# Row pairs folded ahead of the W transform, and both mixings of a spectral block kernel in plain fp32 on 128- and 64-value blocks

## The chip, the core and the metric

The kernel runs on one core of one Trainium2 chip. The metric is device time in microseconds (us) of one launch. Engines are named as in the profile: PE is TensorE, PEld its weight loads, DVE is VectorE, ACT is ScalarE, POOL is GpSimd, SP is the engine that issues most DMAs. Each runs its own instruction list in order, and they meet at semaphores. SBUF is the working memory; PSUM, with 8 banks of 512 fp32 values in each of 128 partitions, takes what PE writes and is not read by POOL.

## The reference

Input x has the shape (4, 128, 128, 768) in fp32: batch, H, W, channels. The 768 channels are 8 blocks of 96, and each block has its own complex 96 x 96 weights.

```python
xf = jnp.fft.rfft2(x, axes=(1, 2), norm='ortho')       # 128 x 65 complex modes
xf = xf.reshape(b, h, wf, NUM_BLOCKS, BLOCK)           # 8 blocks of 96
o1r = relu(xr @ w1[0] - xi @ w1[1] + b1[0])            # the first mixing
o1i = relu(xi @ w1[0] + xr @ w1[1] + b1[1])
o2r = o1r @ w2[0] - o1i @ w2[1] + b2[0]                # the second mixing
o2i = o1i @ w2[0] + o1r @ w2[1] + b2[1]
xc = softshrink(o2r, 0.01) + 1j * softshrink(o2i, 0.01)
out = jnp.fft.irfft2(xc, s=(128, 128), axes=(1, 2), norm='ortho') + x
```

## The kernel before

The work is 32 items, one for each pair of channel block and image (8 x 4). An item is an image of 128 x 128 x 96, which fills one of two buffers `x0` and `x1`, with W on the partitions. The engines loop over 16 steps of two items each (`Fori(0, STEPS)`, the body written out for both items). The order on every engine is written by hand; no scheduler moves anything. An item q goes through five stages on PE.

1. **Forward lines** (`lines(q, p, 0)`, PE line L351). For each of the 96 channels one matmul multiplies a 128 x 128 matrix of x (W by H), as the weights, by the cosine and sine table of W. It goes by 26 groups of up to 4 channels. ACT (L485) or DVE (L592) first packs a group of x, whose values lie 96 apart, into a ring of four slots; after the matmuls ACT (L494) or DVE (L601) moves the group from PSUM to `ydg`.
2. **Mixing**. 22 units of three W frequencies (the first has two). Per unit: `fwd_h` (L372), six matmuls with 96 x 128 weights and 130 columns, transforms H with only 65 of the 128 frequencies, once for the real and once for the imaginary part; DVE puts the full set together from sums and differences (L629 to L632). `mix1` takes three real products in place of four, each of them as three matmuls on numbers split in a high and a low part of type fp32r (L389, L390, L391), for which ACT and POOL make the parts (L513, L519, L734, L743, L746). DVE combines (L652, L655), ACT applies bias and relu (L536). `mix2` (L425, L427) takes two matmuls of 192 columns for each frequency, the bias b2 being a 97th row of the weights. DVE shrinks into `ydg` (L673, L675). At the end `merge` unites W frequencies 0 and 64.
3. **Inverse lines** (`lines(q, p, 1)`, again L351, L485, L494, L592, L601): as the forward ones, with `ydg` as source and destination.
4. **Rows** (`rows`, L445 and L448): 13 groups of two matmuls with up to 480 columns; ACT copies half of the results (L583), DVE and POOL add and subtract them with x (L684, L688, L690, L752) in place.
5. SP stores the buffer in pieces as DVE finishes them, then loads the image after next into it.

In PE's list a plain fp32 matmul is two instructions with a weight load each, a high and a low pass; an fp32r one is a single instruction.

The packing of the next item's first groups stands on ACT behind the last `vcopy` copy of this item, and on DVE behind the last `finish`.

Of the kernel before, what the change touches and what calls it, by code (L numbers as in the profile page):

```python
# [12 lines left out]
NB = 8  # L13
# [3 lines left out]
HS = H // 2 - 1  # L17
KW = W // 2 + 1
# [4 lines left out]


CG = 4
# [5 lines left out]
RING = 4  # L31


def packer(g):
    return "act" if g < 2 or g % 2 == 0 else "dve"


def packed_count(g, who):
    return sum(packer(i) == who for i in range(g + 1))


PACKED = {who: packed_count(NG - 1, who) for who in ("act", "dve")}

KU = 3
NU = 1 + (KW - 2) // KU

# [5 lines left out]
WEIGHT_DMAS = 6  # L52


LAG1, LAG2 = 2, 3


WHOLE = (0, 1)
SPLIT = [v for v in range(NU) if v not in WHOLE]
DVE_SPLITS = (2,)  # L60
POOL_SPLITS = [v for v in SPLIT if v not in DVE_SPLITS]

SUM_LAST = 0

LOW_BANKS = (NU - 3, NU - 1)

# [3 lines left out]
for _name, _n in (("fwd_w", W), ("fwd_h", 2 * HC), ("inv_h", H), ("inv_w_even", W), ("inv_w_odd", W),  # L70
                  ("merge_even", H), ("merge_odd", H)):
    COLS[_name] = (_at, _at + _n)
    _at += _n
TABLE = _at


def transform_table():

# [18 lines left out]
    fwd_w[:, 3::2] = -sin(n, kw)  # L99
    half = np.arange(0, 65)  # L100
    fwd_h = np.concatenate([cos(n, half), sin(n, half)], 1)
# [15 lines left out]
    return np.concatenate([fwd_w / 128, fwd_h, inv_h, inv_even / 128, inv_odd / 128,  # L117
# [3 lines left out]
def build(nc, x, w1, b1, w2, b2, table, out):  # L121
    with ExitStack() as ctx:
# [3 lines left out]
        def sem(name):  # L126
# [3 lines left out]

        xs = [sb(f"x{p}", [W, H, CB]) for p in range(PAIRS)]

        ydg = sb("ydg", [128, 128, CB])


        w1i = sb("w1i", [CB, CB])
        w1g = sb("w1g", [CB, 3, CB])
        w1hi = sb("w1hi", [CB, 3, CB], F32R)  # L140
        w1lo = sb("w1lo", [CB, 3, CB], F32R)
        b1s = sb("b1s", [CB, 2])
        w2r = sb("w2r", [CB + 1, 2, CB])
        w2i = sb("w2i", [CB, 2, CB])
        pcopy = [sb(f"pcopy{j}", [CB, KU, 2 * HC]) for j in range(2)]

        z_or_packed = sb("z_or_packed", [128, 2 * 3 * KU * H])
        z = [z_or_packed[0:CB, j * 3 * KU * H:(j + 1) * 3 * KU * H].rearrange("p (a k n) -> p a k n", a=3, k=KU)
             for j in range(2)]
        packed = [z_or_packed[:, j * CG * 128:(j + 1) * CG * 128].rearrange("p (c k) -> p c k", c=CG)  # L150
                  for j in range(RING)]
# [56 lines left out]


        T_BANK, R_BANK, I_BANK, M_BANK = 2, 3, 4, 5  # L210
        E_BANK = T_BANK

        M_STEP = 320

# [555 lines left out]
```

## Time and profile before

| | us |
|---|---|
| median of 3 runs | 5806.42 (5803.06 to 5810.91) |
| the profiled execution | 5807.0 |
| its span on the core | 5805.2 |
| first matmul of the program, from the span's start | 28.6 |
| PE busy in the span | 5558.5 (96%) |
| DVE, ACT, POOL busy | 4148.0, 3751.7, 3055.2 |

The profiled execution lies 0.6 us above the median, 0.01% of it, so that sums made against the profile can be set against the median as they are. The item's stages repeat 32 times; what one stage costs is read from the start of its first matmul to the start of the next stage's first. A matmul's own duration in the records is longer than the distance to the next one, because matmuls overlap in the array; the distance between starts is what counts.

### The profile page before, as it was taken

What the parts mean: (1) busy time and instruction counts of PE and PEld (TensorE: products, weight loads), DVE (VectorE), ACT (ScalarE), POOL (GpSimd) and SP (SyncE); (2) the same over time, 40 slices, a digit from 0 to 9 for tenths busy, and PEclk for the clock granted to TensorE, in tenths of its full rate; (3) what the DMA queues carried; (4) which work ended last, traced back from release to release, by engine and by line L of the source; (5) the groups of instructions that cost most, each with busy time, mean ns of one, the idle gap of its engine ahead of it and who ended that gap; (6) DMA issues with size and microseconds to landing.
All of it is one profiled execution on the core that took longest, in us unless ns stands there. A gap on an engine that the chain in (4) does not pass through costs nothing.

```text
span 5805.2 us, 115095 instructions
## 1 busy us (share of the span) xinstructions
PE 5558.5 (96%) x36736; PEld 5058.7 (87%) x36736; DVE 4148.0 (71%) x8579; ACT 3751.7 (65%) x6288; POOL 3055.2 (53%) x2420
## 2 busy tenths in 40 slices
PE   7999999999999999999999999999999999999999
PEld 7888988889888898888988888888889888898888
DVE  5777677676777777777777777677776777767676
ACT  5666666666666666666666666666666666666665
POOL 4445564455644556544555446554465544555445
PEclk9999999999999999999999999999999999999999
DMA  4331233312333213332133331333312333123311
GB/s 92 88 89 45 46 88 88 90 48 42 88 88 90 57 38 84 88 90 64 39 76 88 90 72 37 70 88 90 81 37 60 88 90 88 39 51 88 90 45 44
DMA packets 1070797, 413.95 MB, mean 71 GB/s; under 512 B 1069920, under 2 KB 1070048, under 8 KB 1070176
## 3 DMA queue, kind: packets, MB, share of 16 engines
q1 hardware_dynamic: 1070176, 406.13, 29.8%
q8 instruction: 334, 5.47, 0.4%
q14 instruction: 287, 2.35, 0.1%
HBM read 204.76 MB, written 201.33 MB: 70 GB/s over the span
## 4 chain that ended last, share of the span: by engine, by line
PE 82%; issue 12%; DVE 4%; ACT 1%; POOL 1%; DMA 0%; SPq 0%; DVEq 0%; ACTq 0%; POOLq 0%
PE ps L351 20%; PE ps L372 16%; PE ps L425 11%; PE ps L427 11%; PE ps L389 6%; PE ps L390 6%; PE ps L391 6%; PE ps L445 3%; PE ps L448 3%; DVE x L690 2%; PE ps L387 2%; ACT z_or_packed L485 1%; DVE clamped L673 1%; DVE x L688 1%; DVE ydg L601 0%
## 5 line engine op out<-in xcount | busy, mean ns | idle before, releaser
L351 PE MATMUL ps<-tab,z_or_packed 128*128 128x128 f32 x12288 | 1476.1, 285 | 199.3 <-ACT z_or_packed L485 195.1
L351 PEld LDWEIGHTS ps<-tab,z_or_packed 128*128 128x128 f32 x12288 | 1459.0, 200 | 237.7 <-ACT z_or_packed L485 228.6
L752 POOL TENSOR_TENSOR x<-x,vcopy 128x480 f32<-128x480 f32 (+1 forms) x416 | 602.3, 1458 | 1193.4 <-ACT vcopy L583 1191.2
L734 POOL TENSOR_TENSOR z_or_packed<-z_or_packed 96x384 f32<-96x384 f32 (+1 forms) x704 | 696.1, 989 | 971.5 <-DVE z_or_packed L632 583.2
L743 POOL TENSOR_TENSOR zlo<-z_or_packed,zhi 96x768 fp32r<-96x768 f32 x608 | 1107.3, 1821 | 84.8 <-ACT zhi L513 83.8
L673 DVE TENSOR_SCALAR clamped<-ps 128x576 f32<-128x576 f32 (+2 forms) x736 | 530.8, 721 | 755.8 <-PE ps L427 755.8
L372 PE MATMUL ps<-tab,ydg 128*96 128x130 f32 x8192 | 1018.9, 274 | 17.8 <-DVE ydg L601 17.8
L425 PE MATMUL ps<-w2r,hid 97*128 97x192 f32 x4160 | 1019.0, 325 | 0.0
L427 PE MATMUL ps<-w2i,hid 96*128 96x192 f32 x4160 | 1015.1, 325 | 0.0
L372 PEld LDWEIGHTS ps<-tab,ydg 128*96 128x96 f32 x8192 | 971.9, 163 | 30.7 <-ACT ydg L494 23.0
L601 DVE COPY ydg<-ps 128x512 f32<-128x512 f32 (+2 forms) x832 | 549.0, 660 | 542.0 <-PE ps L351 536.2
L536 ACT ACTIVATE hid<-hid,b1s 96x384 f32<-96x384 f32 (+1 forms) x1408 | 780.7, 602 | 66.7 <-DVE hid L652 66.7
L513 ACT CAST zhi<-z_or_packed 96x768 fp32r<-96x768 f32 x640 | 532.6, 832 | 424.9 <-PE ps L391 301.6
L425 PEld LDWEIGHTS ps<-w2r,hid 97*128 97x128 f32 x4160 | 737.4, 189 | 23.2 <-ACT hid L536 5.8
L427 PEld LDWEIGHTS ps<-w2i,hid 96*128 96x128 f32 x4160 | 731.6, 189 | 0.0
L389 PE MATMUL ps<-zhi,w1lo 96*96 96x384 f32 x1920 | 703.6, 366 | 0.0
L746 POOL TENSOR_TENSOR zlo<-z_or_packed,zhi 96x384 fp32r<-96x384 f32 x640 | 649.9, 1016 | 19.9 <-ACT zhi L519 19.9
L390 PE MATMUL ps<-zlo,w1hi 96*96 96x384 f32 x1920 | 646.8, 337 | 0.0
L391 PE MATMUL ps<-zhi,w1hi 96*96 96x384 f32 x1920 | 646.0, 336 | 0.0
L494 ACT COPY ydg<-ps 128x512 f32<-128x512 f32 (+2 forms) x832 | 467.0, 561 | 255.8 <-PE ps L351 255.2
L530 ACT COPY tcopy<-ps 96x384 f32<-96x384 f32 (+1 forms) x704 | 331.5, 471 | 429.1 <-PE ps L391 377.3
L675 DVE TENSOR_TENSOR ydg<-ps,clamped 128x576 f32<-128x576 f32 (+1 forms) x704 | 514.0, 730 | 24.4
(49 smaller groups left out, 7179.3 us busy)
## 6 DMA issues: line engine op xcount, KB each, us to landing
x<-in_x SPq DMA_DIRECT2D x128, 1536.0 KB, 14.9
out<-x SPq DMA_DIRECT2D x352, 480.0 KB, 5.6
out<-x SPq DMA_DIRECT2D x32, 432.0 KB, 4.6
out<-x SPq DMA_DIRECT2D x32, 240.0 KB, 4.3
out<-x SPq DMA_DIRECT2D x32, 192.0 KB, 3.8
w2r<-in_w SPq DMA_DIRECT2D x16, 72.0 KB
w1g<-in_w SPq DMA_DIRECT2D x16, 36.0 KB
w1i<-in_w SPq DMA_DIRECT2D x16, 36.0 KB
```

The source lines that it names most:

```text
L351: mm = pe.matmul(ps[:, bank, j * 128:(j + 1) * 128], packed_slot(stage, g)[:, j, :], rhs, start=True, stop=True)
L372: mm = pe.matmul(ps[0:CB, bank, k * 2 * HC:(k + 1) * 2 * HC], ydg[:, idx, :], mat("fwd_h"), start=True, stop=True)
L389: pe.matmul(o, w1lo[:, j, :], hi, start=True, stop=False)
L390: pe.matmul(o, w1hi[:, j, :], lo, start=False, stop=False)
L391: return pe.matmul(o, w1hi[:, j, :], hi, start=False, stop=True)
L425: pe.matmul(o, hid[v % 2][:, 0, k * H:(k + 1) * H], w2r[:].rearrange("p r c -> p (r c)"), start=True, stop=False)
L427: pe.matmul(o, hid[v % 2][0:CB, 1, k * H:(k + 1) * H], w2i[:].rearrange("p r c -> p (r c)"), start=False, stop=True).then_inc(mix2_done, 1)
L536: ins = act.activation(h, h, ACT.Relu, bias=b1s[:, i:i + 1])
L734: pool.tensor_tensor(zz[:, 0, 0:n, :], zz[:, 2, 0:n, :], zz[:, 1, 0:n, :], ALU.add).then_inc(zsum_ready, 1)
L743: pool.tensor_tensor(lo[:, 1:3, 0:n, :], zz[:, 1:3, 0:n, :], hi[:, 1:3, 0:n, :], ALU.subtract).then_inc(zlo_ready, 1)
L746: pool.tensor_tensor(lo[:, 0, 0:n, :], zz[:, 0, 0:n, :], hi[:, 0, 0:n, :], ALU.subtract).then_inc(zsum_lo_ready, 1)
L752: pool.tensor_tensor(xp, xp, vcopy[g % 3][:, 0:b - a, :], ALU.add).then_inc(plus_ready, 1)
```

## The change

In the forward lines, POOL and DVE take the place of the packing copies: `fold` writes, for each group, the sums of rows h and 128 - h into columns 0 to 63 of a ring slot, and their differences into columns 64 to 126 (the ring has six slots). The two halves go through PE as two matmuls with 64 and 63 weight columns and different tables, which write PSUM partitions 0 to 63 and 64 to 126. So the real H transform has its even and odd part on separate partitions, and afterwards one matmul of 128 weight columns by the new 128 x 128 table `fwd_h` gives all 128 H frequencies of a W frequency. Row 0 has no partner: one matmul of its own, a copy by ACT and two DMAs that ACT issues put it into partition 127.

The split in fp32r parts goes, with its operations on ACT, DVE and POOL, as do the three-product form and the unfolding on DVE. The complex vector of 192 values is now cut in a block of 128 and a block of 64. There are 17 units: 16 of four W frequencies, the last of one. Within a unit two frequencies ("evens") have their 64-blocks on partitions 0 to 63 and two ("odds") on 64 to 127. Matmuls that concern a 64-block use half of the array: 128 x 64 tiles (two column halves) in `fwd_small` and `mix1_columns`, 64 x 128 tiles (two row halves) in `mix1_rows` and `mix2_rows`. All matmuls are plain fp32. b2 is added by DVE. The weights come from one array laid out on the host's side of the launch.

In the inverse lines POOL packs too (as a multiplication by one), and the first six slots are packed in two parts, the large part before the last two units are shrunk.

The first fence is one regular unit of the mixing on PE before (L372 is `fwd_h`, L389 to L391 `mix1`, L425 and L427 `mix2`).

```order
L372 MATMUL ps<-tab,ydg 96x130 x3
L368 REGISTER_ALU
L372 MATMUL ps<-tab,ydg 96x130 x3
L382 REGISTER_ALU
L398 REGISTER_ALU
L389 MATMUL ps<-zhi,w1lo 96x384
L390 MATMUL ps<-zlo,w1hi 96x384
L391 MATMUL ps<-zhi,w1hi 96x384
...
L425 MATMUL ps<-w2r,hid 128x192
L427 MATMUL ps<-w2i,hid 128x192
```

And this is one regular unit now; the size is that of the output, so 64x... stands for a column tile, while L453 and L464 are the row tiles.

```order
L409 MATMUL ps<-tab,ydg 128x128 x4
L436 MATMUL ps<-zbig,wts 128x256 x2
L439 MATMUL ps<-zsmall,wts 128x256
L421 MATMUL ps<-tab,ydg 64x128 x4
L445 MATMUL ps<-zbig,wts 64x256 x2
L453 MATMUL ps<-zsmall,wts 128x256 x2
L464 MATMUL ps<-wts,hsmall 128x192 x4
L472 MATMUL ps<-wts,hbig 128x192 x4
```

A unit of six `fwd_h`, nine `mix1` and six `mix2` matmuls for three frequencies has become one of 23 matmuls for four, in which full matmuls, column tiles and row tiles follow each other in that order.

On DVE, at the end of the mixing and the start of the inverse lines, there stood before the pieces of `shrink` (L673, L675) and then packing and moves. Now three passes stand for each unit, and six short copies of the late columns follow.

```order
L659 TENSOR_TENSOR shrink_or_v<-ps,wts 128x768
L661 TENSOR_SCALAR shrink_or_v<-shrink_or_v 128x768
L669 TENSOR_TENSOR ydg<-shrink_or_v 128x2x2x192
L659 TENSOR_TENSOR shrink_or_v<-ps,wts 128x192
L661 TENSOR_SCALAR shrink_or_v<-shrink_or_v 128x192
L669 TENSOR_TENSOR ydg<-shrink_or_v 128x192
L701 REGISTER_ALU
L704 COPY ring_h<-ydg 128x4x10 x6
```

PE's first inverse matmul waits for the first of the six copies. The core of the diff:

```diff
@@ PE, forward lines
-                        for j in range(LINE_GROUPS[g][1]):
-                            mm = pe.matmul(ps[:, bank, j * 128:(j + 1) * 128], packed_slot(stage, g)[:, j, :], rhs,
+                    pe.wait_ge(y_ready, NF * q + NF - 3)
+                    pe.matmul(ps[:, ROW0_BANK, 0:CB], mat("fwd_w"), xs[p][:, 0, :],
...
+                        for j in range(LINE_GROUPS[g][1]):
+                            o = ps[:, bank, j * 128:(j + 1) * 128]
+                            slot = ring_a[g % RING_A][:, j, :]
+                            pe.matmul(o[0:HALF], slot[:, 0:HALF], mat("fwd_w"), start=True, stop=True)
+                            mm = pe.matmul(o[HALF:127], slot[:, HALF:127], mat("fwd_w_odd"), start=True, stop=True)
@@ fold, on POOL for every third group and the first six, else on DVE
+            engine.tensor_tensor(slot[:, :, 0:HALF], rows(1, HALF + 1), rows(H - 1, HALF - 1, -1), ALU.add)
+            return engine.tensor_tensor(slot[:, :, HALF:127], rows(1, HALF), rows(H - 1, HALF, -1), ALU.subtract)
@@ PE, the mixing
+                        for it in range(NU + 2):
+                            if it < NU:
+                                fwd_big(q, it)
...
+                            if 1 <= it < NU + 1:
+                                mix1_whole(q, it - 1)
+                            if it < NU:
+                                fwd_small(q, it)
+                            if 1 <= it < NU + 1:
+                                mix1_columns(q, it - 1)
+                                mix1_rows(q, it - 1)
+                            if it >= 2:
+                                mix2_rows(q, it - 2)
+                                mix2_whole(q, it - 2)
+                            if it == EDGES + 4:
+                                merge(q)
@@ ACT, row 0
+                    act.copy(row0[:], ps[:, ROW0_BANK, 0:CB]).then_inc(row0_copied, 1)
+                    act.wait_ge(row0_copied, q + 1)
+                    act.dma_start(ydg[127:128, :, :], row0[:]).then_inc(row0_moved, 16)
@@ POOL, after its folds of this item: the first six folds of the next one
+                            pool.wait_ge(x_loaded[1 - p], (t + 1 + p) * 16 * LOADS)
+                            pool.wait_ge(line_done, lines_before(q, 1, 0))
+                            fold_first(1 - p)
@@ ACT, per unit
+                    act.copy(zbig[u % 2][:, 0:n], ps[:, ZBIG_BANK, 0:n]).then_inc(zbig_ready, 1)
...
+                    act.activation(hsmall[u % 2][0:r, 0:n], ps[0:r, SMALL_BANK, 0:n], ACT.Relu, bias=b1[0:r, 1:2])
```

## Rows read from the trace of the kernel before

**Rows 1.** The page: busy time of each engine; then the chain that ended last, by line.

```profile
PE 5558.5 (96%) x36736; PEld 5058.7 (87%) x36736; DVE 4148.0 (71%) x8579; ACT 3751.7 (65%) x6288; POOL 3055.2 (53%) x2420
PE ps L351 20%; PE ps L372 16%; PE ps L425 11%; PE ps L427 11%; PE ps L389 6%; PE ps L390 6%; PE ps L391 6%; PE ps L445 3%; PE ps L448 3%; DVE x L690 2%; PE ps L387 2%; ACT z_or_packed L485 1%; DVE clamped L673 1%; DVE x L688 1%; DVE ydg L601 0%
```

**Rows 2.** Timeline of PE, stages of an item: start, length in us, [idle before].

```profile
929.02 3.17 PE L351 MATMUL ps<-tab,z_or_packed 128*128 128x128 f32 x24 [0.83 <-ACT z_or_packed L485]
932.46 19.02 PE L351 MATMUL ps<-tab,z_or_packed 128*128 128x128 f32 x168 [0.27 <-DVE z_or_packed L592]
952.04 1.98 PE L372 MATMUL ps<-tab,ydg 128*96 128x130 f32 x16 [0.56 <-DVE ydg L601]
...
1058.40 0.49 PE L436 MATMUL ps<-edge,tab 128*128 128x192 f32 x2
1060.78 23.42 PE L351 MATMUL ps<-tab,z_or_packed 128*128 128x128 f32 x192 [1.89 <-ACT z_or_packed L485]
...
1112.02 23.80 PE L351 MATMUL ps<-tab,z_or_packed 128*128 128x128 f32 x192 [6.41 <-ACT z_or_packed L485]
```

**Rows 3.** Timeline of PE inside the mixing: distances between starts.

```profile
1138.20 1.46 PE L387 MATMUL ps<-z_or_packed,w1g 96*96 96x256 f32 x6
...
1150.52 1.49 PE L372 MATMUL ps<-tab,ydg 128*96 128x130 f32 x12
...
1152.21 0.34 PE L391 MATMUL ps<-zhi,w1hi 96*96 96x384 f32 x1
...
1153.44 0.49 PE L425 MATMUL ps<-w2r,hid 97*128 97x192 f32 x2
1153.77 0.49 PE L427 MATMUL ps<-w2i,hid 96*128 96x192 f32 x2
...
1155.40 1.49 PE L372 MATMUL ps<-tab,ydg 128*96 128x130 f32 x12
```

**Rows 4.** Instructions of line L351: count, then min/median/max duration in ns.

```profile
L351 PEld LDWEIGHTS ps<-tab,z_or_packed x12288: 186/192/338, 28.6 to 5771.6; 128*128 128x128 f32 x199
L351 PE MATMUL ps<-tab,z_or_packed x12288: 273/275/583, 28.6 to 5771.8; 128*128 128x128 f32 x199
```

**Rows 5.** Windows: stretch, length, busy time by engine, PEclk the granted clock, DMA.

```profile
1060.00:1064.00 4.00, 3.22 (x18) 3.21 (x19) 0.46 (x2) 4.00 (x5) 0.00 (x0) 0.73 0.18 34
1106.00:1112.00 6.00, 0.00 (x0) 0.00 (x0) 3.55 (x8) 2.37 (x3) 2.52 (x3) 0.80 0.96 249
1112.00:1116.00 4.00, 3.98 (x18) 3.98 (x19) 0.60 (x2) 3.48 (x4) 0.00 (x0) 0.50 1.02 261
```

**Rows 6.** Timeline of all engines around the end of a loop body.

```profile
1108.81 0.54 DVE L690 TENSOR_TENSOR x<-ps,x 128x384 f32<-128x384 f32 x1
...
1109.62 1.28 ACT L485 ACT_TABLE_LOAD   x1 [4.23 <-issue]
...
1111.80 0.64 DVE L592 COPY z_or_packed<-x 128x512 f32<-128x512 f32 x1 [2.45 <-issue]
```

**Rows 7.** Instructions by line and form: count, busy us, mean ns, idle before.

```profile
L752 POOL TENSOR_TENSOR x<-x,vcopy 128x480 f32<-128x480 f32 x352 | 510.7, 1460 | 77.7 <-ACT vcopy L583 75.5
L601 DVE COPY ydg<-ps 128x512 f32<-128x512 f32 x704 | 487.0, 692 | 522.5 <-PE ps L351 521.5
L675 DVE TENSOR_TENSOR ydg<-ps,clamped 128x576 f32<-128x576 f32 x640 | 484.7, 757 | 22.2
L485 ACT COPY z_or_packed<-x 128x512 f32<-128x512 f32 x384 | 413.3, 1093 | 24.5 <-DMA x<-in_x 24.3
L494 ACT COPY ydg<-ps 128x512 f32<-128x512 f32 x704 | 412.4, 586 | 201.2 <-PE ps L351 200.7
L684 DVE TENSOR_TENSOR x<-x,vcopy 128x480 f32<-128x480 f32 x352 | 236.1, 671 | 0.0
L675 DVE TENSOR_TENSOR ydg<-ps,clamped 128x192 f32<-128x192 f32 x32 | 11.4, 358 | 1.1
L734 POOL TENSOR_TENSOR z_or_packed<-z_or_packed 96x384 f32<-96x384 f32 x672 | 673.0, 1001 | 583.2 <-DVE z_or_packed L632 583.2
```

More of the change, by code:

```diff
@@ L74 @@
 TABLE = _at
+FWD = 2 * W
+MIX = {}
+_at = 0
+for _name, _n in (("w1_big", 2 * CB), ("w2_big", 2 * CB), ("w1_small_big", BIG), ("w2_small", 2 * CB),
+                  ("w1_small_small", 2 * SMALL), ("b1", 2), ("b2", 2 * CB)):
+    MIX[_name] = (_at, _at + _n)
+    _at += _n
+MIXED = _at
 def transform_table():
@@ new lines, in fwd_small @@
+                def fwd_small(q, u):
+                    if u:
+                        pe.wait_ge(zsmall_ready, NU * q + u)
+                    for k, pair in enumerate(GROUP_PAIRS[u]):
+                        for i, kw in enumerate(pair):
+                            if kw is not None:
+                                t, s = spectrum(kw)
+                                mm = pe.matmul(ps[i * SMALL:(i + 1) * SMALL, ZSMALL_BANK, k * H:(k + 1) * H],
+                                               t[:, s + 1, CUT:CB], mat("fwd_h"), start=True, stop=True)
+                    mm.then_inc(zsmall_done, 1)
@@ new lines, in mix1_columns, with mix1_rows @@
+                def mix1_columns(q, u):
+                    n, halves = halves_of(u)
+                    for i, a, b in halves:
+                        mm = pe.matmul(ps[i * SMALL:(i + 1) * SMALL, SMALL_BANK, 0:n],
+                                       mix_part("w1_big")[:, BIG:2 * CB], zbig[u % 2][:, a:b], start=False, stop=True)
+                    mm.then_inc(small_mixed, 1)
+                def mix1_rows(q, u):
+                    n, halves = halves_of(u)
+                    for i, a, b in halves:
+                        half = slice(i * SMALL, (i + 1) * SMALL)
+                        mm = pe.matmul(ps[:, BIG_BANK + i, 0:n], mix_part("w1_small_big")[half],
+                                       zsmall[u % 2][half, 0:n], start=False, stop=True)
+                    mm.then_inc(big_mixed, 1)
@@ new lines, in mix2_rows @@
+                def mix2_rows(q, u):
+                    pe.wait_ge(hid_ready, NU * q + u + 1)
+                    if u:
+                        pe.wait_ge(bias_done, NU * q + u)
+                    for k, pair in enumerate(GROUP_PAIRS[u]):
+                        for i in range(2 if pair[1] is not None else 1):
+                            half = slice(i * SMALL, (i + 1) * SMALL)
+                            pe.matmul(ps[:, OUT_BANK + i, k * 2 * CB:(k + 1) * 2 * CB],
+                                      hsmall[u % 2][half, k * H:(k + 1) * H],
+                                      mix_part("w2_small")[half], start=k == 0, stop=False, skip_group_check=True)
@@ new lines, in step @@
+                        for g in range(RING_A, NG):
+                            if packer_a(g) == "pool":
+                                pool.wait_ge(line_done, lines_before(q, 0, g - RING_A) + 1)
+                                fold(pool, p, g).then_inc(folded_pool, 1)
+                        if not (last and p == PAIRS - 1):
+                            pool.wait_ge(x_loaded[1 - p], (t + 1 + p) * 16 * LOADS)
+                            pool.wait_ge(line_done, lines_before(q, 1, 0))
+                            fold_first(1 - p)
```

767 lines of the change are left out of this document (371 added, 396 removed).

## The prediction

> **What bounds the kernel now.** I read the page first: PE is busy for 96% of the span, and the chain that ended last is almost all PE [rows 1]. Busy time alone says little, so I went on to PE's timeline to see whether the matmuls stand as close as they can, and where they don't. In the forward lines 168 records take 19.02 us [rows 2]; less the last one's own length (0.275 us, [rows 4]) that is 0.112 us from start to start for 128 columns. In the mixing, 192 columns take 0.327 us for two records, 0.163 each, and 256 columns 0.217 (1.46 us for six records, less about 0.38 for the last one's own length) [rows 3]. One column costs 0.85 ns in all of them: the array streams without holes, and neither weight loads nor another engine slow it down. One regular unit of the mixing takes 4.88 us (1150.52 to 1155.40) for three frequencies [rows 3].
>
> The holes are between stages [rows 2]. Before the inverse lines PE waits 1.89 us, before the forward lines 0.83 us within a loop body and 6.41 us at its end, 3.6 us on average, always for ACT's packing. After the longer ones the granted clock is at 0.50, which is 1.2 of 2.4 GHz, for some microseconds: 0.73 on average from 1060 to 1064, 0.50 from 1112 to 1116 [rows 5]. So a time can fall in two ways: less array time, or shorter holes.
>
> An item before, from [rows 2]: hole 3.6, forward lines 23.15 (23.80 at the loop's end, 22.5 within), 0.56, mixing 106.8 (952.04 to 1058.89, the end of the merge), 1.89, inverse lines 23.4, 0.56, rows 20.85. That makes 180.8; 32 of them and the 28.6 us of the first load less one hole, plus the last stores, give the span of 5805 to within a few us.
>
> **Forward lines.** Before, 192 PE instructions of 0.112: 21.5 us plus the slow clock. Now 384, as each matmul is two instructions, each still streaming 128 columns. One after the other they would take 43 us. The two halves use different array columns, different PSUM partitions and their own weights, so they can run side by side; the list is first half high, first half low, second half high, second half low. The high pass of the second half can start with the low pass of the first, and the low pass of the second with the next line's high pass. In a long row that is two at a time, 21.5 us again. Row 0 adds 0.2.
>
> The trace shows no tile, so this has two ends: nothing side by side, or all. I take all. The nearest row is that weight loads of 128 columns fit under the same time as the matmul, at 0.112 apart [rows 2, 4]; two loads of 64 columns are as many columns.
>
> The folds feed this. A DVE pass costs 0.36 us for 192 values and 0.76 for 576 [rows 7], so 0.16 plus 1.04 ns a value: 0.43 for 256, 0.85 for a fold. DVE does 13 folds and 6 moves of 0.69: 15.2 us of 21.5. POOL pays 1.00 for 384 values and 1.46 for 480 [rows 7], 2.6 to 3.0 ns a value, so 1.3 to 1.6 for a fold, and has one every third group, that is every 2.7 us. ACT has 20 moves of 0.59, 11.7 us in place of 26 operations up to 1.09. All are hidden under PE. If both strided sources of a fold make it twice as dear, DVE needs 26 us and PE waits for it: a rival below.
>
> **Mixing.** Per unit of four frequencies, by the distances above:
> - `fwd_big` 8 instructions of 0.112: 0.89
> - `mix1_whole` 6 of 0.217: 1.30
> - `fwd_small` 8 of 0.112 one after the other: 0.89. As tiles, with high and low in order, the first high pass and the last low pass stand alone: 5 steps, 0.56, of which the last overlaps with the next group of the same tiling: 0.45
> - `mix1_columns` 4 of 0.217: 0.87; as tiles 3 steps: 0.65
> - `mix1_rows` and `mix2_rows` 4 of 0.217 and 8 of 0.163: 2.18; as tiles 1.30
> - `mix2_whole` 8 of 0.163: 1.31
>
> That is 5.9 us side by side and 7.45 in a row, against 6.5 for four frequencies before. Note that two tiles never reach a half: the staircase of high and low costs 0.5 us a unit. Sixteen units, 95; the last unit, first and last staircases, 2.4; merge 0.65; the fill at the start and the wait of the last `mix2` for DVE's bias pass 1.4: 98.8 + 54 d us, where d is what a change of tiling costs: full, columns, rows, full is three per unit, 54 an item.
>
> **The unknown d.** No row shows a change of tiling. Below: nothing, since [rows 3] show full matmuls of other shape and type (L372, L389 to L391, L425) following each other without any loss (from 1150.52, twelve times 0.112 and two of 384 columns at 0.175 make the 1.69 us to 1152.21). Above: PE must let the last matmul leave the array, 0.163 us (a record of 0.275 less its 0.112), and only then load the new weights, 0.19 for 128 columns and less for 64 [rows 4]: 0.33. I take 0.08, half of the tail alone, since the nearest rows, on changes of shape, say nothing and the tail says 0.16. Then the mixing takes 103.1, 3.7 less than before. The Trainium skill (TensorEngine Tiling (Array Packing), Tiling Modes) says that changing the tiling mode, not just the tile, drains TensorE; it gives no price. By it d would be at least the tail, and the sum comes out at no gain at all; it speaks against this change, and is the first rival. The same skill (TensorE: Matmul & The Clock Gate, Part 3) gives 2.38 times for three column tiles; taking that 0.79 for the tiled 61 us of an item would be an estimate of 16 us more per item, some 6190 us in all. No row here shows either.
>
> The other engines: ACT has per unit a copy of 512 (0.59), two relus (about 0.4 and 0.65): 1.7 us. DVE has a copy (0.43) and three passes of 768 (0.96 each): 3.3. Both are under 6. What POOL and ACT did for the split is gone, and it was hidden, so it brings nothing by itself.
>
> **Into the inverse lines.** Before 1.89 us. Now DVE finishes the unit before the last in 2.9 us (three passes of 768), then does the last one in three passes of 192 (0.36 each, 1.1) and one tail copy; PE's last `mix2` ends 0.75 us behind the start of that. The hole grows to about 3.7: plus 1.8. The other packs are early, on ACT and POOL. Within the inverse lines nothing changes that binds: 23.4.
>
> **Into the forward lines.** POOL has folded the first six groups during the mixing, and row 0 waits for no engine that is late. DVE's last additions, three passes of up to 0.67 us a group [rows 7], free the banks in time. Within a body the hole shrinks from 0.83 to about 0.1. At a body's end each engine pays for the jump: DVE 2.45 us, ACT 4.23 [rows 6]; PE's own was hidden and I take DVE's. Average 1.3 against 3.6, minus 2.3; the slow clock after it is shorter, minus 0.7 less 0.2 for row 0. What hides ACT's jump is that PE has eight banks, some 7 us; what hides DVE's (free at 1111.8 in [rows 6], PE needs its first fold about 6 us after its start) is the six early folds. ACT now issues two DMAs there; they land during 21 us.
>
> **Sum per item**: hole -2.3, forward -0.5, mixing -8.0 + 54 d, inverse hole +1.8: -9.0 + 54 d. With d = 0.08, -4.7; with some 0.5 for the longer slow clock after the larger hole before the inverse lines, -4.2. Times 32, -135 us against the profile's own 5807.0: **5672 us**.
>
> **Rivals.**
> - *The change of tiling drains PE and reloads* (d from 0.165 up). For it: the tail of 0.163 and the loads of 0.19. Against: the order of the calls keeps it to three a unit. d = 0.163 gives 5815, d = 0.33 gives 6100. It decides slower from d = 0.16 on. Chance 0.26.
> - *No cost of changing* (d below 0.03): 5672 less 32 times 4.3, 5534. Chance 0.15.
> - *Tiles don't run side by side*, so the change doesn't do what it says: +21.5 us in the forward lines and 25 in the mixing, 32 times 46.5: some 7160. For it: no row shows two matmuls at once, and every column costs 0.85 ns. Against: their array columns, PSUM partitions and weights are apart. Chance 0.09.
> - *The folds bind*: strided sources at double price, 26.5 us of DVE in the forward lines: +5 per item, 5832. ACT's strided pack costs 1.09 against 0.59 of a move with the same 512 values, which speaks for it; DVE's own strided moves (0.69) speak against. Chance 0.07.
> - *The forecast*, d between 0.03 and 0.15: 5590 to 5790. Chance 0.38. The rest, 0.05, is for no change.
>
> **How the numbers follow.** Faster by over 0.2% (12 us, about what a measurement can tell from none): 0.15 + 0.38 = 0.53. Slower: 0.26 + 0.09 + 0.07 = 0.42. The two sides hold nearly as much, so the likeliest case's own range, 5590 to 5790, stands beside the whole one: from 5510, a little below d = 0, to 6090, which takes in nearly all of the drain rival. Tiles in a row, 0.09, are left out.
>
> **What would show it.** In the profile after, a regular unit of PE between two `fwd_big` takes 5.9 + 3 d; I expect 6.1, 6.4 or more says drain, 7.4 says in a row. Forward lines of 21.7 us within a body say side by side; 43 in a row; 26 with PE waiting for `ring_a` from DVE says folds. The hole before the inverse lines should be 3.7, before the forward lines 0.1 and 2.5. The starts of the first and second half's records should lie 0.056 apart on average. Wrong in another way it would be if the granted clock fell in tiled stretches, where half the array works at a time.

## The result, and the profile after

The changed kernel takes 5840.84 us (median of 5 runs, 5837.85 to 5847.33) against 5806.42: a ratio of 1.0061, with a 95% interval of 1.0047 to 1.0076. It is slightly slower, where 5672 was forecast; the whole range held it, the forecast's own range (5590 to 5790) did not.

The first view is the page of the changed kernel, its busy times and the chain that ended last by engine (compare [rows 1]).

```profile
PE 5407.1 (93%) x44352; PEld 4374.4 (75%) x44352; DVE 3593.4 (62%) x5379; ACT 2044.7 (35%) x3504; POOL 2079.6 (36%) x1572
PE 48%; issue 31%; DVE 12%; POOL 8%; ACT 1%; DMA 0%; SPq 0%; POOLq 0%; DVEq 0%; ACTq 0%
```

Every engine has less to do than before, PE 151 us less, and yet the program is longer. DVE and POOL together have 20% of the chain, where the page of before has 5%, and 82% for PE. The folds are 6 of these 20 (DVE's `ring_a`, L284 and L285); most of the rest is the packing of the inverse lines and the rows. "issue" is time in which the chain waited for nothing that the profile shows. What PE waited for (line, releaser, total us, times, longest):

```profile
PE ps L380 <- DVE ring_a L285: 146.7, 125, 1.7
PE ps L393 <- DVE ring_h L704: 115.0, 32, 3.7
PE ps L380 <- POOL ring_a L285: 32.5, 24, 4.2
```

L380 is the first half of the forward lines and L285 the second pass of a fold: PE now waits for folds. For the stages I took the start of the first and the end of the last PE record of each, as means over all 32 items:

| us per item | before | after | forecast |
|---|---|---|---|
| hole before the forward lines | 3.5 | 0.7 | 1.3 |
| forward lines | 23.15 | **29.94** | 22.6 |
| mixing | 106.7 | 101.5 | 103.1 |
| hole before the inverse lines | 1.9 | 3.6 | 3.7 |
| inverse lines | 23.1 | 23.7 | 23.6 |
| rows, with the small gaps | 22.0 | 22.0 | 22.0 |

The differences add up to 1.1 us an item, and 32 of them to 35, which is the 34.4 us between the medians. The forecast for the forward lines is wrong by over 7 us. These windows of the changed kernel lie in one item's forward lines (busy time of PE, PEld, DVE, ACT, POOL, with counts; then the granted clock):

```profile
764.00:768.00 4.00, 2.07 (x34) 1.89 (x36) 4.00 (x6) 0.22 (x1) 2.40 (x2) 1.00 0.22 41
768.00:772.00 4.00, 3.85 (x67) 3.38 (x62) 4.00 (x7) 1.79 (x4) 2.92 (x2) 1.00 1.08 298
```

DVE is busy for 4.00 of 4.00 us in each, PE for 2.07 and 3.85, at full clock. And this is DVE's timeline in the first of them (start, length):

```profile
764.00 1.50 DVE L284 TENSOR_TENSOR ring_a<-x 128x256 f32<-128x256 f32 x1
765.43 1.45 DVE L285 TENSOR_TENSOR ring_a<-x 128x252 f32<-128x252 f32 x1
...
767.41 0.65 DVE L284 TENSOR_TENSOR ring_a<-x 128x256 f32<-128x256 f32 x1
767.99 0.65 DVE L285 TENSOR_TENSOR ring_a<-x 128x252 f32<-128x252 f32 x1
```

with POOL's timeline at the same time:

```profile
763.68 1.32 POOL L284 TENSOR_TENSOR ring_a<-x 128x256 f32<-128x256 f32 x1
764.97 1.43 POOL L285 TENSOR_TENSOR ring_a<-x 128x252 f32<-128x252 f32 x1
...
769.08 1.72 POOL L284 TENSOR_TENSOR ring_a<-x 128x256 f32<-128x256 f32 x1 [2.68 <-PE ps L381]
```

The same DVE instruction takes 1.50 us while POOL folds and 0.65 after 767.4, when POOL is idle. Over the whole trace a DVE pass of 252 or 256 values takes 0.65 us when POOL is idle. Of all 640 of them 340 take up to 0.8 and 239 over 1.3, up to 1.59. POOL's pass takes 1.06 alone, and mostly 1.3 to 1.5 beside DVE's folds. The price in the prediction was 0.43.

It is not always DVE that is slowed. In the next lines, from the sixth item, DVE's passes stay near 0.7 us while POOL's two take over 4 us each, and then PE waits for POOL. The lines are from the timelines of DVE, POOL and PE:

```profile
951.30 0.73 DVE L284 TENSOR_TENSOR ring_a<-x 128x256 f32<-128x256 f32 x1
...
950.62 4.11 POOL L284 TENSOR_TENSOR ring_a<-x 128x256 f32<-128x256 f32 x1 [4.29 <-PE ps L381]
954.70 4.22 POOL L285 TENSOR_TENSOR ring_a<-x 128x252 f32<-128x252 f32 x1
...
959.06 0.45 PE L380 MATMUL ps<-tab,ring_a 128*64 128x128 f32 x1 [4.16 <-POOL ring_a L285]
```

In 31 of the 32 items at least one of POOL's passes takes over 2 us. The means by form, over all folds of DVE:

```profile
L285 DVE TENSOR_TENSOR ring_a<-x 128x252 f32<-128x252 f32 x320 | 327.2, 1023 | 0.0
L284 DVE TENSOR_TENSOR ring_a<-x 128x256 f32<-128x256 f32 x320 | 313.3, 979 | 70.8 <-PE ps L381 70.7
```

Thirteen folds of 2.0 us and six moves of 0.69 are 30.1 us, and the forward lines take 29.9. That sum is right by chance, and some of the expectations below rest on it. Only ten of the thirteen folds have four channels. By the trace, as a mean over the items, DVE starts its first fold 4.7 us after PE's first forward matmul, because it still adds the last rows of the item before (L677 to L683); its folds and moves then take 24.6 us, and PE ends 0.7 us behind the last of them: 4.7 + 24.6 + 0.7 = 30.0.

So my theory was: **the folds are the bound, at a price that has two parts, the strided sources and POOL beside DVE.** The rivals were that PE is limited by its tiles or by the changes of tiling there too, that POOL's folds are late on their own account, and that ACT's moves or the banks hold PE up.

### The profile page after: what moved, and what is told of

The parts are those of the page before. It is cut to its first block, busy times and chain, and to the rows that moved or that the text cites. A ratio compares the mean times of both kernels' runs of the same rounds, so it can differ in the third digit from the quotient of the medians.

```text
span 5838.6 us, 114567 instructions
## 1 busy us (share of the span) xinstructions
PE 5407.1 (93%) x44352; PEld 4374.4 (75%) x44352; DVE 3593.4 (62%) x5379; ACT 2044.7 (35%) x3504; POOL 2079.6 (36%) x1572
## 4 chain that ended last, share of the span: by engine, by line
PE 48%; issue 31%; DVE 12%; POOL 8%; ACT 1%; DMA 0%; SPq 0%; POOLq 0%; DVEq 0%; ACTq 0%
PE ps L472 8%; PE ps L393 6%; PE ps L409 6%; PE ps L436 5%; PE ps L453 4%; POOL ring_h L719 4%; PE ps L464 4%; PE ps L421 3%; DVE ring_a L285 3%; DVE x L683 3%; DVE ring_a L284 3%; PE ps L445 3%; PE ps L439 3%; PE ps L380 2%; POOL x L746 2%
## 5 line engine op out<-in xcount | busy, mean ns | idle before, releaser
L719 POOL TENSOR_TENSOR ring_h<-ydg,ones 128x512 f32<-128x512 f32 (+1 forms) x320 | 426.0, 1344 | 3056.4 <-DVE ydg L669 2653.5
L659 DVE TENSOR_TENSOR shrink_or_v<-ps,wts 128x768 f32<-128x768 f32 (+1 forms) x544 | 501.2, 921 | 1323.3 <-PE ps L472 1323.3
L537 ACT COPY ydg<-ps 127x512 f32<-127x512 f32 (+6 forms) x1056 | 581.6, 562 | 993.5 <-PE ps L381 571.1
L380 PE MATMUL ps<-tab,ring_a 128*64 128x128 f32 x6144 | 756.4, 282 | 183.5 <-DVE ring_a L285 146.7
L380 PEld LDWEIGHTS ps<-tab,ring_a 128*64 128x64 f32 x6144 | 698.1, 142 | 235.6 <-issue 172.9
L393 PE MATMUL ps<-tab,ring_h 128*128 128x128 f32 x6144 | 757.9, 290 | 115.0 <-DVE ring_h L704 115.0
L393 PEld LDWEIGHTS ps<-tab,ring_h 128*128 128x128 f32 x6144 | 751.8, 206 | 124.4 <-DVE ring_h L704 124.4
L472 PE MATMUL ps<-wts,hbig 128*128 128x192 f32 x4160 | 821.6, 340 | 0.0
L381 PE MATMUL ps<-tab,ring_a 128*63 128x128 f32 x6144 | 762.0, 283 | 0.0
L472 PEld LDWEIGHTS ps<-wts,hbig 128*128 128x128 f32 x4160 | 661.0, 189 | 122.3 <-issue 122.3
L284 POOL TENSOR_TENSOR ring_a<-x 128x256 f32<-128x256 f32 (+1 forms) x416 | 561.8, 1350 | 408.6 <-DMA x<-in_x 223.4
L746 POOL TENSOR_TENSOR x<-x,shrink_or_v 128x480 f32<-128x480 f32 (+1 forms) x416 | 601.6, 1456 | 284.9 <-ACT shrink_or_v L605 282.4
L381 PEld LDWEIGHTS ps<-tab,ring_a 128*63 128x63 f32 x6144 | 697.2, 141 | 0.0
L409 PE MATMUL ps<-tab,ydg 128*128 128x128 f32 x4032 | 549.6, 276 | 21.0 <-ACT ydg L537 21.0
L409 PEld LDWEIGHTS ps<-tab,ydg 128*128 128x128 f32 x4032 | 518.1, 191 | 39.2 <-issue 39.2
L669 DVE TENSOR_TENSOR ydg<-shrink_or_v 128x768 f32<-128x768 f32 (+2 forms) x544 | 533.5, 981 | 17.8
L285 POOL TENSOR_TENSOR ring_a<-x 128x252 f32<-128x252 f32 (+1 forms) x416 | 520.8, 1252 | 0.0
L464 PE MATMUL ps<-wts,hsmall 64*128 64x192 f32 x4160 | 439.1, 324 | 36.5 <-DVE shrink_or_v L659 36.5
```

What stands on the lines that cost most here:

```text
L284: engine.tensor_tensor(slot[:, :, 0:HALF], rows(1, HALF + 1), rows(H - 1, HALF - 1, -1), ALU.add)
L285: return engine.tensor_tensor(slot[:, :, HALF:127], rows(1, HALF), rows(H - 1, HALF, -1), ALU.subtract)
L380: pe.matmul(o[0:HALF], slot[:, 0:HALF], mat("fwd_w"), start=True, stop=True)
L381: mm = pe.matmul(o[HALF:127], slot[:, HALF:127], mat("fwd_w_odd"), start=True, stop=True)
L393: mm = pe.matmul(ps[:, line_bank(1, g), j * 128:(j + 1) * 128], ring_h[g % RING_H][:, j, :], mat("inv_h"), start=True, stop=True)
L409: mm = pe.matmul(ps[:, ZBIG_BANK, k * H:(k + 1) * H], t[:, s:s + 2, :].rearrange("p k c -> p (k c)")[:, 0:BIG], mat("fwd_h"), start=True, ...
```

## Experiments on the folds

**Is it the folds at all?** All folds but the six early ones were cut to one channel; PE reads old values for the others, so this kernel leaves out work.

```diff
@@ fold
+            n = n if g < RING_A else 1
```

> Work left out: from the seventh group on, fold writes one of the up to four channels, and PE reads old values for the others; all waits and matmuls stay. Theory (the folds bind): the forward lines fall to what the matmuls take, 21.5 to 22 us, and the whole to 5841 - 32 x 8 = 5585 us. Rival (tiled matmuls are slower by themselves, by weight loads or issue): the stage stays near 29.9 and the time near 5840.

Measured: 5593.16 us, ratio 0.9639 (0.9623 to 0.9655). The forward lines fall to 22.0 us, and what PE waits for has no fold among its larger entries. Everything else keeps its length to 0.2 us (mixing 101.5, hole 3.6). So the folds' price is the whole difference between 5841 and 5593, and tiles, banks and moves are not what limits the forward lines. Which engine's folds, and by what, this does not tell. It is also what the forecast would have been worth with free folds.

**Which engine's?** First DVE's six moves were given to ACT, to leave DVE the folds alone.

```diff
@@ mover, stage 0
-        return "dve" if g % 4 == 3 else "act"
+        return "act"
```

> DVE no longer moves any forward group out of PSUM; ACT moves all 26. Theory (DVE's own list sets the forward lines: 13 folds of 2.0 us and 6 moves of 0.69 make the 29.9 us): the stage falls by 4.1 us to about 25.8, times 32 that is 130 us, 5710 us. Rival (POOL sets it, or PE's tiled matmuls): the stage stays at 29.9 and the time at 5840. ACT has 26 times 0.59, 15.3 us, and should not bind in either.

Measured: 5847.82, ratio 1.0074 (1.0055 to 1.0094), no gain at all. Four us of DVE's work went, and the forward lines still took 29.6. What PE waited for in this kernel:

```profile
PE ps L380 <- DVE ring_a L285: 88.8, 86, 1.7
PE ps L380 <- POOL ring_a L285: 61.6, 23, 5.0
```

The waits for DVE fell by 58 us, those for POOL rose by 29. A DVE pass still takes 0.98 us on average, and the longest single pass of POOL takes 9.4 us, where the changed kernel has 4.3. The hole at the end of a loop body grew from 1.6 to 2.9 us, 15 times, which takes back some 20 us, more than the 0.4 us an item that the forward lines gained. This miss made me look at the two engines together.

**POOL's folds taken away from POOL.**

```diff
@@ packer_a
-    return "pool" if g % 3 == 0 or g < RING_A else "dve"
+    return "pool" if g < RING_A else "dve"
```

> POOL folds only the six early groups, DVE all 20 others. Theory (a DVE fold costs 1.30 us when POOL is idle, and is slowed to up to 2.9 by POOL's fold beside it): 20 times 1.30 and 6 moves of 0.69 make 30.2 us, as good as the 29.9 of now: 5850 us, and the records of L284 and L285 on DVE all at 0.65. Rival (the strided fold costs 1.0 per pass in any case, as the mean of now says): 20 times 2.0 and 4.1 make 44 us, 6290 us.

Measured: 5820.27, ratio 1.0033 (1.0019 to 1.0048). DVE has seven folds more, and the kernel is faster than the changed one. Nearly all of its folds now take about what they took alone. The form of DVE's first pass (count, busy us, mean ns):

```profile
L284 DVE TENSOR_TENSOR ring_a<-x 128x256 f32<-128x256 f32 x512 | 351.6, 687 | 73.3 <-PE ps L381 67.8 <-issue 5.5
```

and DVE's timeline, to set beside the 1.50 above:

```profile
764.01 0.68 DVE L284 TENSOR_TENSOR ring_a<-x 128x256 f32<-128x256 f32 x1
764.58 0.69 DVE L285 TENSOR_TENSOR ring_a<-x 128x252 f32<-128x252 f32 x1
765.15 0.71 DVE L622 COPY ydg<-ps 127x512 f32<-127x512 f32 x1
```

From start to start that is some 0.58 a pass. POOL's help in the forward lines was worth less than what it took from DVE, by 20.6 us in all.

**Both edits together.**

> Both edits together: DVE folds all 20 groups after the six early ones, ACT moves all 26. Theory (DVE and POOL folds share one path, so that a POOL fold takes from DVE what it gives; moves out of PSUM don't use it): DVE has 25.0 us of folds (16 full ones at 1.35 and the short ones) and nothing else, the forward lines fall from 29.1 to 25 us, and the whole from 5820 to about 5690 us, below the kernel before. Rival (moving the moves to ACT brings nothing, as when POOL folded too): 5820 us.

Measured: 5748.91, ratio 0.989 (0.9872 to 0.9908); forward lines 26.1. The hole at a loop body's end grew to 2.9 us, as in the kernel with the moves on ACT; that cost some 20 us (1.3 us, 15 times), a third of what was missed, and no run shows what PE waits for there. The rest is in the forward lines, and the trace shows where: DVE starts its first fold 4.1 us after PE's first matmul (3.7 within a body), behind the last rows of the item before; its folds, 16 of four channels and four short ones, then take 21.4 us, and PE ends 0.6 us later. PE's groups start 1.15 us apart there, DVE's pace, where PE alone needs 0.87. The view of PE's waits shows nothing of this, as each of these waits is short.

**And two more early folds on POOL**, which runs them during the mixing: `RING_A` 6 to 8.

> As e5, with eight ring slots and eight early folds on POOL in place of six. Theory (DVE's list of folds sets the forward lines): two folds of 1.35 us less, forward lines from 25 to 22.5 us, some 80 us less than e5, about 5610 us. Rival (something else binds once the moves are gone): as e5.

Measured: 5673.06, ratio 0.9759 (0.9741 to 0.9776); forward lines 24.4, by 1.65 less, where two folds of 1.16 are 2.3. Missed by 63 us: the loop's end again, and DVE's late start, which the expectation had left out. It shows that the folds still bind with DVE by itself: from DVE's first fold to its last it is 19.3 of the 24.4 us, and 4.5 pass before.

**The strides.** In the change a fold reads both sources with values 384 bytes apart and writes one run. Here it walks channels innermost, so that four values of each source lie together, and the ring is written 128 values apart.

```diff
@@ fold
-            slot = ring_a[g % RING_A][:, 0:n, :]
+            slot = ring_a[g % RING_A][:, 0:n, :].rearrange("p c h -> p h c")
...
-                return xs[p][:, a:b:step, c:c + n].rearrange("p h c -> p c h")
+                return xs[p][:, a:b:step, c:c + n]
...
-            engine.tensor_tensor(slot[:, :, 0:HALF], rows(1, HALF + 1), rows(H - 1, HALF - 1, -1), ALU.add)
+            engine.tensor_tensor(slot[:, 0:HALF, :], rows(1, HALF + 1), rows(H - 1, HALF - 1, -1), ALU.add)
```

> Same folds on the same engines, walked with h outside and the four channels inside: sources in runs of four values, the slot written 128 values apart. If the fold's price of 1.9 ns a value on DVE comes from its two sources being read 96 values apart: DVE alone falls from 0.65 to about 0.43 us a pass and the forward lines from 29.9 to about 22, 5590 us. If single values cost it on the writing side as well: no gain, 5840 us; if that costs more, slower.

Measured: 5647.82, ratio 0.9715 (0.9698 to 0.9732), by 193 us less than the change, with no work taken away. The forms of DVE's folds:

```profile
L285 DVE TENSOR_TENSOR ring_a<-x 128x252 f32<-128x252 f32 x320 | 270.6, 846 | 0.0
L284 DVE TENSOR_TENSOR ring_a<-x 128x256 f32<-128x256 f32 x320 | 240.0, 750 | 68.4 <-PE ps L381 65.7 <-issue 2.7
```

Alone a DVE pass still takes 0.61, so DVE by itself gained little; a POOL pass went from 1.06 to 0.73, and beside it DVE takes some 1.1 in place of 1.5. So the order of the walk acts through POOL and through the time in which both run.

**The strides off DVE's output too.** The ring is laid out [W, 128, 4], so that a fold reads and writes runs of four, and PE takes its weights 16 bytes apart.

```diff
-        ring_a = [sb(f"ring_a{j}", [W, CG, 128]) for j in range(RING_A)]
+        ring_a = [sb(f"ring_a{j}", [W, 128, CG]) for j in range(RING_A)]
...
-                            slot = ring_a[g % RING_A][:, j, :]
+                            slot = ring_a[g % RING_A][:, :, j]
```

> The same walk, and the ring slots laid out with the channel innermost, so that the fold writes one run and PE loads its weights with a step of four values. Theory (sources read 96 apart make the price): a DVE pass at 0.43 us, 5590 us, if PE's weight loads don't care about the step; if they do, the forward lines show PEld records above 0.142 us and the stage is set by PE. Rival (price not from the stride): 5840 us.

Measured: 5655.08, ratio 0.9731 (0.9713 to 0.9748): no better than the last one, against 5590 expected. The folds did as expected: DVE's pass takes 0.41 alone, near the 0.43 that the prediction had from rows of contiguous data, and PE waits 2.2 us for folds in the whole program. But the weight loads of L380 rose, here this kernel's row and then that of the changed one:

```profile
L380 PEld LDWEIGHTS ps<-tab,ring_a 128*64 128x64 f32 x6144 | 747.2, 209 | 5.9 <-POOL ring_a L285 3.0
```

```profile
L380 PEld LDWEIGHTS ps<-tab,ring_a 128*64 128x64 f32 x6144 | 698.1, 142 | 235.6 <-issue 172.9 <-ACT ydg L537 47.2 <-POOL ring_a L285 9.9
```

The layout moved the cost of the stride from DVE to PE. PE's pairs now start 0.120 us apart, evenly through the stage, where they started 0.109 apart; over 192 pairs that is 2.1 us, and the forward lines take 24.0 us, where 22.0 is possible, while PE waits for almost nothing.

**The best of these.** The walk with channels innermost, and eight slots.

> e6 (the fold walked with the channels inside) with eight ring slots and early folds. e6's forward lines took 23.6 us, 1 us of it waiting for DVE's folds; with two folds less they should be at PE's 21.9: 32 x 1.5, 5600 us. Rival (something else holds them at 23.6): 5648 us.

Measured: **5603.3 us** (5601.99 to 5604.94), ratio 0.9657 (0.9641 to 0.9673) against the kernel before, and 4.1% under the changed one. Forward lines 22.3 us, 21.5 within a body. What PE waits for most, and what is left for the folds:

```profile
PE ps L393 <- DVE ring_h L704: 115.1, 32, 3.7
...
PE ps L380 <- DVE ring_a L285: 5.6, 13, 0.5
PE ps L380 <- POOL ring_a L285: 3.6, 6, 0.8
```

All folds together come to 9 us. The largest wait left is that before the inverse lines. With the moves on ACT as well:

> e10 with ACT moving all forward groups. If the lines are at PE's pace in e10 already, this brings nothing there and loses some 0.6 us an item at the loop's end, as e5 and e1 did (the hole before row 0 grew from 1.6 to 2.9 us there): 5620 us. If DVE still bound in e10: below it, 5590 us.

Measured: 5627.11, ratio 0.97 (0.9684 to 0.9716), 24 us more, as expected: the forward lines are the same (22.3), the hole at a loop body's end is 2.8 in place of 1.5, which makes some 20 us over the 15 ends. The view names a pass of DVE's rows for it:

```profile
PE ps L364 <- DVE x L683: 31.6, 11, 2.9
```

That is hardly the cause: DVE's passes lie at the same distances behind PE's rows in both kernels, the named one ending at 2.1 us, and without the edit PE starts at 1.5, before that pass has ended. With it PE starts at 2.8; why, no run shows.

## Experiments on the tiles

First the regular unit of the mixing on PE in the changed kernel (start, length, count):

```profile
1000.80 1.05 PE L409 MATMUL ps<-tab,ydg 128*128 128x128 f32 x8
1001.69 1.03 PE L436 MATMUL ps<-zbig,wts 128*128 128x256 f32 x4
1002.56 0.59 PE L439 MATMUL ps<-zsmall,wts 128*128 128x256 f32 x2
1003.09 0.66 PE L421 MATMUL ps<-tab,ydg 128*64 128x128 f32 x8
1003.57 0.60 PE L445 MATMUL ps<-zbig,wts 128*64 128x256 f32 x4
1004.10 0.70 PE L453 MATMUL ps<-zsmall,wts 64*128 64x256 f32 x4
1004.64 0.82 PE L464 MATMUL ps<-wts,hsmall 64*128 64x192 f32 x8
1005.39 1.57 PE L472 MATMUL ps<-wts,hbig 128*128 128x192 f32 x8
1006.79 1.05 PE L409 MATMUL ps<-tab,ydg 128*128 128x128 f32 x8
```

The unit takes 5.99 us. Two tiles at a time, without any staircase, the streams of [rows 3] add up to 0.89 + 1.30 + 0.44 + 0.43 + 0.43 + 0.65 + 1.31 = 5.45. The other 0.54 stands where the tiling changes: from L439 to the second columns group L445 it is 1.01 for 0.87 of stream, on to L464 1.07 for 0.86, on to the next L409 2.15 for 1.96. That is 0.14 for full to columns, 0.21 for columns to rows, 0.19 for rows to full, some 0.18 each. The unit alone can't tell this from other losses at those places, so one kernel has five changes a unit in place of three, with the same matmuls:

```diff
+                            if it < NU:
+                                fwd_small(q, it)
                             if 1 <= it < NU + 1:
                                 mix1_whole(q, it - 1)
-                            if it < NU:
-                                fwd_small(q, it)
```

> Same matmuls, but fwd_small stands between fwd_big and mix1_whole: two more changes of tiling per unit, and its last low pass no longer overlaps with mix1_columns (0.11 a unit). If a change costs d = 0.03 us, as the unit of 5.99 us says: +0.17 a unit, +2.8 us an item, 5930 us. If a change drains the array (0.16 us): +0.43 a unit, +7.3 us an item, 6075 us. If a change costs nothing: 5900 us.

Measured: 6031.85, ratio 1.0391 (1.0374 to 1.0408), between the 5930 and the 6075 that were expected for 0.03 and for 0.16 us a change, and nearer the second. Its unit:

```profile
1001.41 1.16 PE L409 MATMUL ps<-tab,ydg 128*128 128x128 f32 x8
1002.50 0.66 PE L421 MATMUL ps<-tab,ydg 128*64 128x128 f32 x8
1003.09 1.13 PE L436 MATMUL ps<-zbig,wts 128*128 128x256 f32 x4
...
1007.85 1.05 PE L409 MATMUL ps<-tab,ydg 128*128 128x128 f32 x8
```

It takes 6.44 us, so five changes cost 0.99, 0.20 each, and the two added ones 0.45. The mixing of an item is 107.0 us, 5.5 more, which is 176 of the 191 us between the two kernels.

The prediction had taken it that high and low pass of one half stand in order, so that two halves make a staircase. The forward lines of the changed kernel show something else, here the first pairs after row 0:

```profile
756.86 0.46 PE L364 MATMUL ps<-x,tab 128*128 128x96 f32 x2 [1.77 <-issue]
757.25 0.32 PE L380 MATMUL ps<-tab,ring_a 128*64 128x128 f32 x1
757.26 0.32 PE L381 MATMUL ps<-tab,ring_a 128*63 128x128 f32 x1
757.41 0.27 PE L380 MATMUL ps<-tab,ring_a 128*64 128x128 f32 x1
757.42 0.27 PE L381 MATMUL ps<-tab,ring_a 128*63 128x128 f32 x1
757.52 0.27 PE L380 MATMUL ps<-tab,ring_a 128*64 128x128 f32 x1
757.52 0.27 PE L381 MATMUL ps<-tab,ring_a 128*63 128x128 f32 x1
```

The list has two instructions of L380 and then two of L381; the records have them alternate from the first on, under 0.01 us apart, and a pair every 0.11. To see how far this goes, one kernel puts four of one half (eight instructions) ahead of four of the other, with the thin folds of the first experiment, whose 5593 is the comparison:

```diff
-                            pe.matmul(o[0:HALF], slot[:, 0:HALF], mat("fwd_w"), start=True, stop=True)
-                            mm = pe.matmul(o[HALF:127], slot[:, HALF:127], mat("fwd_w_odd"), start=True, stop=True)
...
+                            pe.matmul(ps[0:HALF, bank, j * 128:(j + 1) * 128], ring_a[g % RING_A][:, j, 0:HALF],
+                                      mat("fwd_w"), start=True, stop=True)
+                        for j in range(LINE_GROUPS[g][1]):
+                            mm = pe.matmul(ps[HALF:127, bank, j * 128:(j + 1) * 128],
...
```

> As e3 (folds of one channel from the seventh group on, so that PE alone sets the forward lines; work left out as there), with PE's list reordered in every group: first the four matmuls of columns 0 to 63, then the four of columns 64 to 127. Theory (each tile takes its matmuls from a stretch of the list, as the pairs of the trace show, which start 6 ns apart although the list has high and low of one half first): pairs stay side by side if the stretch reaches over 16 instructions; the forward lines stay at 22 us, 5593 us. Rival (strictly in the order of the list): seven of eight steps of a group run alone, 42 us, 6200 us. A value between tells how far the stretch reaches.

Measured: 5685.52, ratio 0.9802 (0.9786 to 0.9819), between the two expectations and much nearer the first. The forward lines take 24.85 us, 2.8 more than with the halves in turns, against some 43 if everything stood in a row. From its timeline, at the start of the forward lines (lines L379 and L382 are the two halves):

```profile
735.21 0.76 PE L379 MATMUL ps<-tab,ring_a 128*64 128x128 f32 x5
735.70 0.32 PE L382 MATMUL ps<-tab,ring_a 128*63 128x128 f32 x1
735.81 0.27 PE L379 MATMUL ps<-tab,ring_a 128*64 128x128 f32 x1
735.86 0.27 PE L382 MATMUL ps<-tab,ring_a 128*63 128x128 f32 x1
```

Five instructions of the first half stand alone, and then the second half's, eight places behind in the list, go beside it. So PE takes matmuls of another tile ahead of earlier ones of its own, by some places; how many, and by what rule, one kernel doesn't settle.

## Why the prediction was wrong, point by point

**The step that failed is the term for DVE's work in the forward lines.** "0.16 plus 1.04 ns a value: 0.43 for 256, 0.85 for a fold", 15.2 us in all with the moves, and "all are hidden under PE". A DVE pass took 0.65 alone and up to 1.59 beside POOL, 1.0 on average, so a fold of four channels 2.0. DVE's folds and moves took 24.6 us in place of 15.2, and began 4.7 us late. Four things were off.

- *Strides.* The rows behind the price ([rows 7], L675 with 192 and 576 values) have one source in PSUM and one in SBUF, both in runs. A fold reads two sources in SBUF, both 96 values apart. A pass took 0.41 with sources and output in runs of four, 0.61 with the output alone strided, and 0.65 with both sources strided. The prediction weighed this as a rival, against DVE's strided move at 0.69 for 512; but that move has one source, in PSUM.
- *Two engines at once.* The prediction never asked what POOL does to DVE, or DVE to POOL. DVE passes with a PSUM source are not slowed: in the changed kernel L659 (PSUM source, 768 values) takes 957 ns whether POOL works or not. L669, from and to SBUF, takes 958 alone, 1690 beside POOL's folds and 1870 beside its packing (L719). The Trainium skill (SBUF — State Buffer, Who interferes with whom) has it: a DVE instruction with two SBUF inputs contends with a GpSimd instruction that reads SBUF. The trace agrees, with these times of L669 and those of the folds, both of which take their two inputs from SBUF.
- *POOL's own price.* It was put at 1.3 to 1.6 us a fold, one every 2.7 us. Two passes of 1.06 are 2.1 alone, and beside DVE they are 3.1 on average, which is no longer hidden.
- *DVE's start.* The sum gave DVE the whole stage. It first folds 4.7 us into it, behind the last rows of the item before. The six early folds hide that from PE at the start, but the time is missing later.

The trace of the kernel before had the second point, though not in the means of [rows 7]. DVE's L684 and POOL's L752 run side by side in the rows, and both read two SBUF sources. POOL's line there (count, min/median/max in ns):

```profile
L752 POOL TENSOR_TENSOR x<-x,vcopy x416: 1197/1453/1745, 186.0 to 5793.8; 128x480 f32<-128x480 f32 x117, 128x384 f32<-128x384 f32 x22
```

The shortest and the longest are the same addition of 480 values. L684 ran beside most of the shortest for 0.1 us and beside the longest for over 0.6, and over all of them POOL's pass grows by 1.0 us for each us of L684 beside it. DVE's own pass took 0.64 to 0.66 us in 320 of 352 cases, so there it was POOL that paid, and some 0.9 in the other 32; in the folds either of the two pays.

How the parts share the loss is an estimate. With DVE's pace of 0.58 us a pass from the kernel in which it folds alone, its thirteen folds and six moves take some 17 us; with the late start that ends near 22 us, where PE needs 21.5 to 22. By that the strides and the late start use up the cover, and most of the 8 us comes from the two engines together.

Put into the prediction's own sum, 1.0 us a pass gives 13 x 2 x 1.0 + 4.1, or 30 us, which looks like the 29.9 measured. It is luck: that sum counts three small folds as full ones and leaves out the late start.

The rival "the folds bind" named 5832 us, with a chance of 0.07, and its mechanism is what happened. That its number comes within 9 us is luck too: 26.5 us of DVE was forecast there from doubled strides alone, the stage took 29.9, and the holes and the mixing gave the rest back. Its chance was too low, since its own sentence had a row that spoke for it (ACT's strided pack at 1.09 for 0.59) and the cover was thin: of DVE's 15.2 us in 21.5 the folds were 11.1, so a price 1.6 times as high uses it up, before POOL does anything.

**What was right.** The holes: 3.6 us before the inverse lines against 3.7, by the same three passes of DVE; 0.7 before the forward lines against 1.3. Tiles run side by side: the forward lines at 22.0 with thin folds, and 21.5 within a body at the best. The longer slow clock in the inverse lines: 0.6 against 0.5. The rows: nothing. The clock: 1.00 in the stretches of the forward lines above, and 1.00 from 790 to 860 us in the mixing. With thin folds the kernel stands at 5593, 79 us under the forecast: 1.6 us an item in the mixing and some 0.6 each in the forward lines and the hole before them, 2.8 times 32, or 90.

**Right by two errors that cancel: the mixing.** 101.5 against 103.1. The staircase of 0.5 us a unit isn't there, and a change of tiling costs 0.18, not 0.08. The first was worth -8 us an item, the second +5.4. The tail of 0.163, named as the lower end of the drain rival, is what the change costs, and not the tail and the load on top of it, 0.33. The Trainium skill says that changing the tiling mode drains TensorE (TensorEngine Tiling (Array Packing), Tiling Modes). The trace agrees, in that each change costs 0.14 to 0.21 us, about the tail. By the prediction's own sum a d of 0.163 gives 5815 and the measured 0.18 some 5845; the kernels without a fold bound stand at 5593 to 5603, because the staircase, 8 us an item or 256 in all, went.

**What stays open.** Why DVE alone still takes 0.61 us when only the output is strided, where [rows 6] have 0.64 for a copy of 512 values (L592); what decides whether DVE or POOL is slowed when both fold; by which rule PE takes matmuls of another tile ahead; and why the hole at a loop body's end grows by 1.3 us when ACT does all moves of the forward lines. The hole of 3.6 us before the inverse lines, 115 us of the program, was not tried.

## What to carry to other kernels

Before work is moved from one engine to another "because it is hidden there", price it from a row with the same strides and the same memories as sources, and ask which other engine works on SBUF at that time: here these made 0.43 us into 1.0, and 15 us of DVE's work under 21.5 of PE's into 24.6. Ask too when that engine is free to begin: here it was 4.7 us into the stage. A mean can hide that two engines slow each other; look at the shortest and the longest of the same instruction. If helping engines slow each other, an early share (two more slots, filled during another stage) is worth more than a share at the same time. When a layout is turned to spare one engine, look at whoever reads it next: the ring that made folds fast made weight loads slow, and it was the walk, with the two more slots, and not the layout, that gave the 3.4%.

## What the runs showed of the hardware

- DVE and POOL passes with two SBUF sources slow each other. For fp32 additions of 252 or 256 values, strided, DVE's pass goes from 0.65 us to as much as 1.59, POOL's from 1.06 mostly to 1.3 to 1.5 and at times to over 4 (9.4 in the kernel with the moves on ACT). POOL's addition of 480 values takes 1.20 to 1.75 us, by how long DVE's L684 runs beside it. A DVE copy of 512 values from SBUF to SBUF (L616) goes from 0.66 to 1.00 beside POOL's packing. DVE passes with a PSUM source were not slowed (957 ns both ways).
- An fp32 addition of 256 values takes 0.41 us on DVE with sources and output in runs of four values, 0.61 with the output 512 bytes apart, 0.65 with both sources 384 bytes apart; on POOL 0.73 with runs in the sources, 1.06 without.
- Two column tiles of TensorE start under 0.01 us apart although the list has two passes of one ahead of two of the other, and a pair of 128 columns takes 0.11 us, the time of one. With eight of one tile ahead of eight of the other they still overlap, at a loss of 2.8 us in 26 groups.
- A change between full array, column tiles and row tiles costs 0.14 to 0.21 us.
- A weight load of 64 columns takes 142 ns from values that lie together, 209 ns from values 16 bytes apart; pairs of matmuls then start 0.120 us apart in place of 0.109.
